# Writing out the group loop of an image-tower kernel on four engines

## The chip, the cores and the metric

The kernel runs on one core of a Trainium2 chip. The metric is the device time of one execution in microseconds (us), and of several runs the median. The core has four compute engines with an instruction stream each, TensorE (PE, the matrix unit), VectorE (DVE), ScalarE (ACT) and GpSimd (POOL), and SyncE (SP), which here issues most of the DMAs. Each stream is a program of its own: it has its own waits on semaphores, and its own branches if it has a loop.

## What is computed

Sixteen images of 3 x 256 x 256 pixels go through three steps:

```python
h = sum over channels of hypot(sobel_x(x), sobel_y(x))        # 16 x 256 x 256
h = concatenate([cls_tok, h])                                  # 257 tokens of 256 channels
y = layernorm(h)
h = h + attention(y)    # the 27 tokens of the greatest norm ask, 16 heads, all 257 answer;
                        # the other tokens get the mean of y
z = layernorm(h)
h = h + bit_linear(silu(depthwise_conv1d(bit_linear(z, w1))), w2)
```

`bit_linear` rounds its input to 8 bits row by row and its weights to -1, 0 and 1. The order of the additions and the roots are followed closely, so the gradient's length alone takes a chain of about 25 VectorE operations for two rows of pixels.

## The kernel before

The sixteen images are taken in four groups of four (`GROUPS = 4`, `GB = 4`). 128 partitions hold four images, 32 blocks of rows each; a partition has eight rows (`ROWS`), which are done in four pairs (`PAIRS`).

The work is software-pipelined over the groups. A head computes the gradients of group 0 and its norm. Then a **group loop** runs three passes (g = 1, 2, 3). A pass computes the gradients and the norm of group g, and between their steps the attention and the feed-forward part of group g - 1. A tail does attention and feed-forward of group 3. I call them pass 1, pass 2 and pass 3.

The loop stands in four streams, each with a counter in a register and a branch back at its end: on DVE (L1143), ACT (L1522), PE (L1828), and on SP (L457), where it has two passes only, since SP's first and last group are written out. GpSimd's stream has no loop. There is no barrier at the end of a pass: the streams meet only at semaphores. A semaphore counts up over the whole kernel, so inside the loop the value to wait for depends on the pass. It is worked out in a register, as in `Chain.__call__` (L107 to L111), which is used behind nearly every VectorE operation:

```python
    def __call__(self, ins):
        self.n += 1
        ins.then_inc(self.sem, 1)
        if self.n > self.lag:
            self.eng.wait_ge(self.sem, self.base + self.n - self.lag)
```

`base` is a number outside the loop and an expression of the register g inside it. The profile lists these register operations as ALU_OP and FUSED_REGOPS.

On DVE a pass is: `first_rows` (L1066, two operations on the image, L1069), `magnitude_rows` of pairs 0 and 1 with the attention of the previous group put in their slots (`slots_0`, `slots_1`), `attend`, `magnitude_rows` of pairs 2 and 3, `ffn_quantize`, `norm_tokens`, `ffn_result`. The last instruction of a pass is a one-column memset in `settle` (L521), which fills a gap; it writes the next free column of the scratch tile `idle`, which has 48. `selected_tokens` (L983) waits for the matmuls that gather the selected tokens (L1726), `own_heads` (L1014) for the weighted values (L1776, L1777), and `hypotenuse` starts with a wait for ACT's absolute values (L1238).

On ACT a pass begins with L1227, on PE with `attention` (L1701), after the copies of the transposed tokens (L1394). On SP a pass loads the next group's images, reloads weights, takes the token norms to DRAM and back, stores the previous group's output (`store`, L452, L454), and carries the slot numbers (L439 to L446).

A second, smaller loop of two passes in the tail (L1180 on DVE, L1549 on ACT) is not touched.

Of the kernel before, what the change touches and what calls it, by code (L numbers as in the profile page):

```python
# [44 lines left out]
GROUPS = B // GB  # L45
# [76 lines left out]
def tower_kernel(nc, x, cls_tok, w_in, b_qk, b_v, w_out, b_out, w1, conv_w, conv_b, w2, const, out):  # L122
# [9 lines left out]
    with ExitStack() as ctx:  # L132
# [238 lines left out]
        def load_rows(queue, g, b, lo, hi_, landed):  # L371

            block_rows, first = (slice(0, BLK), lo) if lo < ROWS else (slice(1, BLK + 1), lo - ROWS)
            src = x[bass.ds((g * GB + b) * CH, CH), block_rows, first:first + hi_ - lo, :].rearrange("c p r w -> p c r w")
            for c in range(CH):
                queue.dma_start(img[b * BLK:(b + 1) * BLK, c, lo:hi_, :], src[:, c]).then_inc(landed, 16)

        def load_images(queue, g):

            for b in range(GB):  # L380
                load_rows(queue, g, b, 0, ROWS, img_in)
                load_rows(queue, g, b, ROWS, ROWS + 2, img_in)
# [4 lines left out]
        @block.sync  # L387
        def _(sp):
            def load_weights():
                sp.dma_start(win[:, :, :], w_in.rearrange("(t p) n -> p t n", p=P)).then_inc(weights_in, 16)  # L390
                sp.dma_start(wout[:, :, :], w_out.rearrange("(t p) n -> p t n", p=P)).then_inc(weights_in, 16)

            for b in range(0, GB, 2):
                load_rows(sp, 0, b, 0, 3, img_first)
            sp.dma_start(cst[:, :], const).then_inc(table_in, 16)
            for b in range(0, GB, 2):
                load_rows(sp, 0, b, 3, 4, img_second)
            for b in range(GB):
                load_rows(sp, 0, b, 4, ROWS, img_in)
                load_rows(sp, 0, b, ROWS, ROWS + 2, img_in)  # L400
            sp.dma_start(h9[:, ROWS, :], cls_tok[0:1, :].to_broadcast([P, D])).then_inc(const_in, 16)
            sp.dma_start(stage.rearrange("p (t n) -> p t n", t=DT),
                         w1.rearrange("(t p) n -> p t n", p=P)).then_inc(w1_in, 16)
            sp.dma_start(stage2.rearrange("p (t n) -> p t n", t=FT),
                         w2.rearrange("(t p) n -> p t n", p=P)).then_inc(w2_in, 16)
            load_weights()
            sp.dma_start(bin_col[:, :], b_qk).then_inc(const_in, 16)
            sp.dma_start(bv_col[:, :], b_v).then_inc(const_in, 16)
            sp.dma_start(bo_row[:, :], b_out[0:1, :].to_broadcast([P, D])).then_inc(const_in, 16)
            sp.dma_start(cw[:, :, :], conv_w).then_inc(const_in, 16)  # L410
            sp.dma_start(cb[:, :], conv_b).then_inc(const_in, 16)

            def group(g, first=False, last=False):
                if first:
                    sp.wait_ge(stencil_psum, 2 * ROWS - 3)
                elif not last:
                    sp.wait_ge(mags, g * (2 * PAIRS) + 2 * PAIRS)
                if not last:
                    load_images(sp, g + 1)
                if not first:  # L420

                    sp.wait_ge(f_ready, g * GB)
                    load_weights()
                if first:

                    sp.wait_ge(e_ready, 1)
                    sp.dma_start(ec_dram, e9[0:1, ROWS:ROW9]).then_inc(e_out, 16)
                    sp.wait_ge(e_out, 16)
                    sp.dma_start(topk[:, 0, 0:1], ec_dram.to_broadcast([GB, 1])).then_inc(erow_in, 16)

                sp.wait_ge(e_ready, g + 1)
                sp.dma_start(e_dram, e9[:, 0:ROWS]).then_inc(e_out, 16)
                sp.wait_ge(e_out, g * 16 + 32)
                sp.dma_start(topk[:, 0, 1:S], e_dram.rearrange("(b r) j -> b (r j)", b=GB)).then_inc(erow_in, 16)
                if not first:
                    store(g - 1)

                sp.wait_ge(slots_ready, g + 1)
                sp.dma_start(s_dram.rearrange("(b r) j -> b (r j)", b=GB), topk[:, 4, 1:S]).then_inc(slots_out, 16)  # L439
                if not first:  # L440

                    sp.wait_ge(out_done, g * OUT_DONE)
                sp.dma_start(c_dram.rearrange("(b r) o -> b (r o)", b=GB), clsslot[:, :]).then_inc(slots_out, 16)
                sp.wait_ge(slots_out, g * 32 + 32)
                sp.dma_start(slot9[:, 0:ROWS], s_dram).then_inc(slot9_in, 16)
                sp.dma_start(slot9[:, ROWS:ROW9], c_dram).then_inc(slot9_in, 16)  # L446

            def store(g):

                sp.wait_ge(out_ready, g + 1)  # L450
                for b in range(GB):
                    sp.dma_start(out[bass.ds(g * GB + b, 1), 1:S, :].rearrange("o (p r) d -> (o p) r d", r=ROWS),  # L452
                                 out9[b * BLK:(b + 1) * BLK, 0:ROWS, :]).then_inc(out_done, 16)
                sp.dma_start(out[bass.ds(g * GB, GB), 0, :], out9[0:P:BLK, ROWS, :]).then_inc(out_done, 16)  # L454

            group(0, first=True)
            with sp.Fori(1, GROUPS - 1) as g:  # L457
                group(g)
            group(GROUPS - 1, last=True)
            store(GROUPS - 1)  # L460
            sp.wait_ge(out_done, GROUPS * OUT_DONE)
# [51 lines left out]
        def _(dve):  # L513
            v = nc.vector

            settled = [0]

            def settle():

                settled[0] += 1  # L520
                v.memset(idle[:, settled[0]:settled[0] + 1], 0.0)  # L521

            def bc(a, n):
# [57 lines left out]
            def norm_mean(step, rows, g):  # L581

                mean = small[:, 0, 0:rows]
                dve.wait_ge(rows_done, g * ROWS + ROWS + 2)
                ordered_sum(step, rows, h9[:, 0:rows, :], 16, mean)
                step(v.tensor_scalar(mean, mean, -1.0 / D, None, ALU.mult))
# [475 lines left out]
            def norm_tokens(step, g, rows, before_y=None):  # L1062
                norm_rows(step, rows, g * 2 + 1, before_y)
                dve.wait_ge(e_ready, g + 1)

            def first_rows(step, g):  # L1066
                dve.wait_ge(img_in, g * IMG_IN + IMG_IN)
                for f in range(2):
                    step(negative_edge_row(edge[:, f], f))  # L1069
                settle()  # L1070
# [69 lines left out]
            assert norm_step.n == NORM_STEPS - 1, norm_step.n  # L1140

            with dve.Fori(1, GROUPS) as g:  # L1143
                gl = g - 1
                norm_step = Chain(dve, vnorm, g * NORM_STEPS - 1)
                step = Chain(dve, vstep, gl * G_STEPS)
                first_rows(norm_step, g)
                magnitude_rows(g, 0, slots_0(step, gl))
                magnitude_rows(g, 1, slots_1(step, gl))
                attend(step, gl)  # L1150
                settle()
                for j in range(2):
                    magnitude_rows(g, 2 + j, lambda k: None)

                ffn_quantize(step, gl, range(GB), lambda: norm_mean(norm_step, ROWS, g),
                             lambda: norm_variance(norm_step, ROWS, g * 2 + 1))
                norm_tokens(norm_step, g, ROWS, lambda: dve.wait_ge(o_psum, gl * 5 + 5))
                ffn_result(step, gl)
                assert (norm_step.n, step.n) == (NORM_STEPS, G_STEPS), (norm_step.n, step.n)
# [32 lines left out]
        def _(act):  # L1192
# [326 lines left out]
                s.activation(clsT[:, t:t + 1], (A0, A1)[t][:, 0:1], ACT.Copy).then_inc(clsT_taken, 1)  # L1519

            tokens_transposed(0)
            with act.Fori(1, GROUPS) as g:  # L1522
                gl = g - 1
                magnitude_rows(g, 0, slots_0(gl))
                magnitude_rows(g, 1, slots_1(gl))
                attend(gl)
                tap_diagonals(gl)
                for j in range(2):
                    magnitude_rows(g, 2 + j, lambda k: ffn_take(gl, j, k))
                norm_squares(lambda j: ln[0][:, j, :], d_ready, g, ROWS)  # L1530
                ffn_scales(gl)
                first_root(g, ROWS)
                hidden_codes(gl)
                second_root(g, ROWS)
                tokens_transposed(g)
# [21 lines left out]
        def _(pe):  # L1557
# [267 lines left out]

            transposed(0)
            pe.wait_ge(bo_ready, 1)
            with pe.Fori(1, GROUPS) as g:  # L1828
                attention(g - 1)
                feed_forward(g - 1, convolve=True)  # L1830
                transposed(g, g * 5)
# [46 lines left out]
```

## Time and profile before

| | |
|---|---|
| median of 3 runs | 1610.13 us (1609.64 to 1610.77) |
| profiled execution, its own time | 1608.93 us |
| its span, first to last instruction | 1607.1 us |
| VectorE busy | 1383.6 us, 86% |
| TensorE matmul busy | 814.8 us, 51% |
| ScalarE busy | 700.1 us, 44% |
| mean granted TensorE clock | 0.706 |

The profile is of one execution, and its times run from the first instruction of the program. Register operations and branches do not count as busy time. "Idle before, issue" means that an engine stood still and no semaphore or transfer that the profile knows ended the wait. The clock is the share of full speed that TensorE was granted: 1.0 is 2.4 GHz, 0.5 is 1.2 GHz.

### The profile page before, as it was taken

What the parts mean: (1) busy time and instruction counts of PE and PEld (TensorE: products, weight loads), DVE (VectorE), ACT (ScalarE), POOL (GpSimd) and SP (SyncE); (2) the same over time, 40 slices, a digit from 0 to 9 for tenths busy, and PEclk for the clock granted to TensorE, in tenths of its full rate; (3) what the DMA queues carried; (4) which work ended last, traced back from release to release, by engine and by line L of the source; (5) the groups of instructions that cost most, each with busy time, mean ns of one, the idle gap of its engine ahead of it and who ended that gap; (6) DMA issues with size and microseconds to landing.
All of it is one profiled execution on the core that took longest, in us unless ns stands there. A gap on an engine that the chain in (4) does not pass through costs nothing.

```text
span 1607.1 us, 12610 instructions
## 1 busy us (share of the span) xinstructions
PE 814.8 (51%) x3262; PEld 639.7 (40%) x3262; DVE 1383.6 (86%) x2154; ACT 700.1 (44%) x1252; POOL 110.1 (7%) x154
## 2 busy tenths in 40 slices
PE   3466002465466733466447743356527754388543
PEld 1233001354354632355336532344426643276433
DVE  7999998999789999899879999899879999622676
ACT  2322241354456633254375544155356663143562
POOL 0000000010202000001101000002100100000000
PEclk7777556767579866667569876577568976677876
DMA  7001500030404510013303510104211300100001
GB/s 194 7 7 26 99 0 1 0 63 10 73 1 69 102 40 4 24 21 51 62 10 59 112 39 0 28 0 72 47 25 26 47 15 25 27 0 0 1 1 26
DMA packets 33976, 56.82 MB, mean 35 GB/s; under 512 B 6602, under 2 KB 23930, under 8 KB 32250
## 3 DMA queue, kind: packets, MB, share of 16 engines
q0 software_dynamic: 21024, 29.11, 11.2%
q1 hardware_dynamic: 12314, 26.31, 7.2%
q10 hardware_dynamic: 576, 0.79, 0.2%
q14 instruction: 49, 0.40, 0.1%
q8 instruction: 13, 0.21, 0.1%
HBM read 22.84 MB, written 4.25 MB: 17 GB/s over the span
## 4 chain that ended last, share of the span: by engine, by line
DVE 31%; issue 27%; ACT 15%; PE 12%; DMA 1%; DVEq 0%; SPq 0%; ACTq 0%
DVE arena L534 9%; DVE arena L531 6%; PE psum L1776 2%; ACT arena L1317 2%; DVE arena L903 2%; PE psum L1726 2%; PE psum L1630 1%; PE psum L1777 1%; PE psum L1812 1%; DVE red L547 1%; ACT arena L1453 1%; ACT arena L1200 1%; PE psum L1748 1%; DVE others L534 1%; ACT zT L1462 1%
## 5 line engine op out<-in xcount | busy, mean ns | idle before, releaser
L531 DVE TENSOR_TENSOR arena<-arena 128x768 f32<-128x768 f32 (+2 forms) x537 | 489.6, 967 | 24.8 <-ACT arena L1238 23.1
L534 DVE SCALAR_TENSOR_TENSOR arena<-arena 128x768 f32<-128x768 f32 (+2 forms) x224 | 201.5, 949 | 0.1
L1644 PE MATMUL psum<-zT,w1q 128*128 128x257 f32 x512 | 151.6, 435 | 40.9 <-ACT wout L1347 24.9
L1644 PEld LDWEIGHTS psum<-zT,w1q 128*128 128x128 f32 x512 | 112.1, 222 | 67.4 <-issue 27.3
L1630 PE MATMUL psum<-gpad,win 128*128 128x257 f32 x288 | 84.7, 437 | 54.6 <-ACT gpad L1329 54.6
L1269 ACT ACTIVATE arena<-arena 128x768 f32<-128x768 int16 x32 | 27.0, 843 | 174.9 <-DVE arena L534 174.4
L534 DVE SCALAR_TENSOR_TENSOR arena<-img 128x768 f32<-128x768 f32 x92 | 83.1, 950 | 16.4 <-DMA img<-x 8.6
L1748 PE MATMUL psum<-arena 128*128 128x257 f32 x128 | 51.0, 566 | 86.9 <-ACT arena L1436 65.7
L1630 PEld LDWEIGHTS psum<-gpad,win 128*128 128x128 f32 x288 | 62.3, 221 | 71.5 <-ACT gpad L1329 60.7
L507 POOL DMA_DIRECT2D h<-others x60 | 51.7, 862 | 404.4 <-DVE others L534 332.9
L1200 ACT ACTIVATE arena<-arena 128x256 f32<-128x256 f32 x65 | 23.3, 409 | 121.0 <-DVE arena L534 68.2
L1748 PEld LDWEIGHTS psum<-arena 128*128 128x128 f32 x128 | 34.8, 285 | 98.5 <-issue 83.8
L903 DVE TENSOR_REDUCE arena<-arena 128x288 f32<-128x2304 f32 (+1 forms) x16 | 64.5, 4086 | 0.1
L479 POOL DMA_DIRECT2D arena<-nrows_mem x18 | 15.6, 902 | 696.9 <-ACT arena L1248 533.4
L1776 PE MATMUL psum<-arena 128*128 128x64 f32 x256 | 55.0, 354 | 11.8 <-ACT arena L1436 11.8
L1426 ACT ACTIVATE arena<-psum,arena 128x257 f32<-128x257 f32 x64 | 29.5, 474 | 71.1 <-DVE arena L1002 71.1
L1336 ACT ACTIVATE xT<-psum,cb 128x257 f32<-128x257 f32 x96 | 43.6, 477 | 36.3 <-PE psum L1630 36.1
L534 DVE SCALAR_TENSOR_TENSOR arena<-arena,others 128x768 f32<-128x768 int16 x64 | 58.2, 949 | 0.0
L1726 PE MATMUL psum<-onehot,arena 128*128 128x128 f32 x128 | 24.2, 366 | 62.9 <-DVE arena L979 62.9
L1776 PEld LDWEIGHTS psum<-arena 128*128 128x128 f32 x256 | 47.7, 256 | 19.5 <-ACT arena L1436 13.6
L1317 ACT ACTIVATE arena<-xT 128x2048 f32<-128x2048 f32 (+1 forms) x14 | 55.3, 3951 | 0.3
L531 DVE TENSOR_TENSOR arena<-arena,img 128x768 f32<-128x768 f32 x59 | 53.9, 950 | 0.5
(225 smaller groups left out, 1980.7 us busy)
## 6 DMA issues: line engine op xcount, KB each, us to landing
img<-x SPq DMA_DIRECT2D x36, 258.0 KB, 6.9
h<-others POOLq DMA_DIRECT2D x60, 128.0 KB, 2.7
arena<-nrows_mem POOLq DMA_DIRECT2D x18, 384.0 KB, 4.4
arena<-arena POOLq DMA_DIRECT2D x18, 384.0 KB, 4.1
arena<-img POOLq DMA_DIRECT2D x18, 384.0 KB, 4.9
out<-out SPq DMA_DIRECT2D x16, 256.0 KB
img<-x SPq DMA_DIRECT2D x48, 64.5 KB, 5.9
win<-w_in SPq DMA_DIRECT2D x4, 768.0 KB, 5.5
```

The lines of the kernel that those rows point to most:

```text
L507: pool.dma_start(h9[:, row, :], others[:, row % 2, c, :], accum_op=ALU.add).then_inc(row_sums, 16)
L531: return v.tensor_tensor(o, a, b, op)
L534: return v.scalar_tensor_tensor(out=o, in0=a, scalar=s, in1=b, op0=op0, op1=op1)
L903: return v.tensor_reduce(fmax[:, :, bass.ds(b, 1), :].rearrange("p j o r -> p j (o r)"), f4[:, :, :, bass.ds(b, 1), :].rearrange("p t j o ...
L1200: ins = s.activation(ln[1][:, j, :], src(j), ACT.Square)
L1317: s.activation(fb[:, :, 0:ROWS, :], yd[:, :, 1:S].rearrange("p t (r j) -> p t j r", j=ROWS), ACT.Silu)
L1336: s.activation(ydw[:, t, :], (C0, C1, T0, T1)[i % 4][:, 0:S], ACT.Identity, bias=cb[:, t:t + 1]).then_inc(conv_taken, 1)
L1630: ins = mm((C0, C1, T0, T1)[i % 4][:, 0:S], diagonal(t, k), gpad[:, i % 4, k:k + S], start=(k == 0), stop=(k == 2))
L1644: ins = mm((A0, A1, B0, B1)[i % 4][:, 0:S], w1q[:, k, t * P:(t + 1) * P], zT[:, k, b, :], start=(k == 0), stop=(k == DT - 1))
L1726: ins = mm(C0[:, t * P:(t + 1) * P], y_row(j)[:, t * P:(t + 1) * P], rhs, start=(j == 0), stop=(j == ROWS))
L1748: mm((C0, C1, T0, T1)[hg][:, 0:S], qbd[:, hg // 2, 4 * (hg % 2):4 * (hg % 2) + 4, :].rearrange("p h q -> p (h q)"), kT[:, b % 2, hg // 2, ...
L1776: mm(B1[:, chans], attnT[:, f, m, cols], V[:, b % 2, m, chans], start=(m == 0), stop=False)
```

## The change

The three passes of the group loop are generated by a Python loop while the program is built, in place of a loop on the chip. Every pass has its own instructions then, and g is a number: each semaphore value and each address that was worked out in a register becomes a constant. The register operations, the counter and the branch back are gone from these four streams. Which compute operations and transfers there are, their order in each stream, and what each waits for stay as they were. Since `settle` is now called more often while the program is built, its column wraps around inside the 48 columns of `idle`.

```diff
@@ sync
             group(0, first=True)
-            with sp.Fori(1, GROUPS - 1) as g:
+            for g in range(1, GROUPS - 1):
                 group(g)
@@ vector
             def settle():
 
-                settled[0] += 1
+                settled[0] = settled[0] % 46 + 1
                 v.memset(idle[:, settled[0]:settled[0] + 1], 0.0)
@@ vector
-            with dve.Fori(1, GROUPS) as g:
+            for g in range(1, GROUPS):
                 gl = g - 1
@@ scalar
-            with act.Fori(1, GROUPS) as g:
+            for g in range(1, GROUPS):
                 gl = g - 1
@@ tensor
-            with pe.Fori(1, GROUPS) as g:
+            for g in range(1, GROUPS):
                 attention(g - 1)
```

## Rows read from the trace of the kernel before

**Rows 1.** The page, busy time, share of the span and instructions

```profile
PE 814.8 (51%) x3262; PEld 639.7 (40%) x3262; DVE 1383.6 (86%) x2154; ACT 700.1 (44%) x1252; POOL 110.1 (7%) x154
```

**Rows 2.** Windows: pass 1, pass 2, pass 3, tail; busy time, PE clock, DMA

```profile
274.40:641.30 366.90, 192.37 (x807) 157.07 (x808) 339.60 (x517) 178.19 (x329) 32.52 (x42) 0.72 0.22 39
641.30:1013.70 372.40, 198.73 (x803) 161.23 (x803) 339.56 (x517) 177.82 (x327) 32.53 (x42) 0.70 0.23 41
1013.70:1385.90 372.20, 199.55 (x804) 161.76 (x804) 339.65 (x517) 177.83 (x327) 32.53 (x42) 0.70 0.17 31
1385.90:1607.00 221.10, 132.97 (x598) 107.89 (x596) 111.13 (x235) 90.10 (x167) 0.00 (x0) 0.75 0.04 10
```

**Rows 3.** Timeline of DVE where a pass begins: start, length, [idle before <-releaser]

```profile
273.94 0.06 DVE L521 MEMSET idle<- 128x1 f32 x1
274.48 1.95 DVE L534 SCALAR_TENSOR_TENSOR arena<-img 128x768 f32<-128x768 f32 x2 [0.48 <-issue]
...
641.23 0.06 DVE L521 MEMSET idle<- 128x1 f32 x1
644.68 1.95 DVE L534 SCALAR_TENSOR_TENSOR arena<-img 128x768 f32<-128x768 f32 x2 [3.39 <-issue]
...
1385.83 0.25 DVE L521 MEMSET idle<- 128x1 f32 x2
```

**Rows 4.** The loop's line L1143: its branch, ns min/median/max

```profile
L1143 DVEq COMPARE_BRANCH  x3: 55/63/63, 641.3 to 1385.9; - x3
```

**Rows 5.** Instruction fetches by DMA queue: packets, MB; pass 1 (two rows), then pass 2

```profile
q8 instruction: 6, 0.10, 0.1%
q14 instruction: 12, 0.10, 0.1%
...
q14 instruction: 14, 0.11, 0.1%
```

**Rows 6.** Waits of DVE in pass 1 (two rows) and pass 2 (four): total, times, longest

```profile
DVE arena L531 <- PE psum L1777: 5.6, 1, 5.6
DVE arena L983 <- PE psum L1726: 0.5, 1, 0.5
...
DVE arena L531 <- PE psum L1777: 7.8, 2, 5.6
DVE arena L531 <- ACT arena L1238: 7.7, 2, 5.6
DVE arena L534 <- issue: 3.4, 1, 3.4
DVE arena L983 <- PE psum L1726: 1.4, 1, 1.4
```

**Rows 7.** Timeline of ACT and of PE where pass 2 begins

```profile
652.87 1.71 ACT L1227 ACTIVATE arena<-arena 128x768 f32<-128x768 f32 x2 [10.02 <-DVE arena L531]
...
642.98 3.36 PE L1701 MATMUL psum<-xT,win 128*128 128x257 f32 x7 [0.77 <-ACT xT L1394]
```

**Rows 8.** Timeline of SP in pass 2: the store, the slot numbers

```profile
641.38 2.75 SPq L452 DMA_DIRECT2D out<-out  x4
...
661.76 0.28 SPq L439 DMA_DIRECT2D s_dram<-nrows_mem  x1
```

**Rows 9.** Timeline of DVE at a wait that takes two register operations

```profile
327.34 0.17 DVE L1008 RECIPROCAL arena<-arena 128x4 f32<-128x4 f32 x1
327.54 0.42 DVE L531 TENSOR_TENSOR arena<-cst,arena 128x256 f32<-128x256 f32 x1
328.09 0.76 DVE L531 TENSOR_TENSOR arena<-arena,cst 128x256 f32<-128x256 f32 x2
```

**Rows 10.** Windows of the gathering matmuls (L1726): two of pass 1, one of pass 2

```profile
297.00:300.20 3.20, 2.94 (x14) 2.95 (x15) 3.20 (x5) 0.00 (x0) 0.00 (x0) 0.51 0.00 0
300.20:303.00 2.80, 2.80 (x27) 2.80 (x27) 2.26 (x4) 1.40 (x2) 0.00 (x0) 1.00 0.00 0
...
667.50:672.20 4.70, 4.69 (x22) 4.69 (x23) 4.70 (x6) 0.37 (x1) 0.00 (x0) 0.50 0.00 0
```

## The prediction

> **What bounds the kernel now.** I read the page first. VectorE is busy for 86% of the span, no other engine for more than 51% [rows 1]. That is an average, so the next view is the windows, cut at the points where the group loop begins, turns and ends. In each of the three passes VectorE works 339.6 us of 367 to 372, which is 91 to 93%; in the tail it works only 111 of 221 us and waits for PE and ACT [rows 2]. The passes make up 1111 of the 1607 us, and in them a microsecond of VectorE's time is a microsecond of the kernel's unless a later wait takes it back. The reader should also see that the three passes do the same work (517 VectorE instructions, 339.6 us each), yet the first is 5.5 us shorter than the second and the third [rows 2]. So this trace already holds an experiment: whatever the passes differ by is idle time.
>
> The third view is VectorE's timeline where a pass begins. Pass 1 is entered from above: the engine is idle for 0.48 us between the last memset and the first operation on the image. Pass 2 is entered by the branch back: 3.39 us idle, and pass 3, at 1017.05, has the same row with the same 3.39. The cause is given as "issue", so that no semaphore or transfer ended it. Where the loop is left by not branching, two memsets of 0.06 us take 0.25 us together, so some 0.13 us of it is idle [rows 3]. The branch itself is listed with 0.06 us at all three ends [rows 4]. The cost is therefore not in executing the branch but in what follows when it is taken: the stream has to begin again at instructions that it left hundreds of instructions ago. The DMA queues show that instructions are fetched from memory all the time, 12 packets in pass 1 and 14 in pass 2 on the queue that VectorE uses [rows 5].
>
> The Trainium skill says this outright (Runtime: NRT & Kernel Launch, section Instruction fetch mechanics): the sequencer streams instructions forward through two blocks, and a taken branch to a target outside of them must fetch it before anything goes on. The trace agrees: 3.39 us where the branch is taken, 0.13 us where it is not.
>
> **The change, part by part.**
>
> *The branch back on DVE.* Removed are three starts of a pass: 0.48 + 3.39 + 3.39 = 7.26 us, of which a straight stream should keep about 0.03 us each, the gap that stands between dependent operations elsewhere [rows 3, 9]. That is 7.2 us. The exit gives 0.1 us. Sum: 7.3 us.
>
> *The register operations on DVE.* Most are free: they run while the operation before them, usually one of 0.95 us, still computes. They cost something only behind a short operation and where two follow each other. The first operation of `queries` is such a place: 0.13 us idle against 0.03 us between the two operations ahead of it [rows 9]. There are three of these in each pass, for images 1, 2 and 3, so 9 x 0.10 = 0.9 us. Bounds: nothing, if the chain through PE and ACT that starts there ends later anyway, and 2 us if a few single gaps of the same size that I have not counted go too. I take 0.9.
>
> *The branches back on ACT and PE.* Cost nothing today, gain nothing. ACT's first operation of pass 2 starts at 652.87 after a wait of 10.02 us for VectorE's gradient, and PE's first starts when ACT has copied the last transposed tokens [rows 7]. What hides ACT's restart is VectorE's own start of the pass. After the change the gradient comes some 3.4 us earlier, and 10.0 - 3.4 = 6.6 us of cover are left, even if ACT's branch were still there.
>
> *SP.* It loses its branch and the register work ahead of each DMA. It is past four stores within 2.75 us, and the slot numbers that VectorE asks for leave at 661.76 [rows 8]. This transfer waits for VectorE's selection, so it moves up with it. Ahead of it on SP's queue stands a wait until the stores have landed. They were issued by 645.3; moving the selection up by 3.4 us leaves 13 us for them. Hidden on both sides, so 0, at most 0.1 us per pass.
>
> *More instructions to fetch.* PE's blocks were fetched six times in pass 1, and the queue is not listed at all in pass 2: its loop stayed on the chip [rows 5]. After the change passes 2 and 3 fetch them too, about 12 more packets. Price: nothing if they run ahead of PE, as in pass 1, which is the shortest pass. From above I have only the nearest row, 3.39 us for a fetch that nothing covers [rows 3]. I take 0, since pass 1 fetched for all engines and lost nothing by it.
>
> *The wrapped column of `idle`.* The same memset elsewhere: 0.
>
> *Where the time goes next.* When VectorE comes 3.4 us earlier into a pass, its partners come earlier too, since they wait for it. The waits that remain in a pass are chains that begin and end on VectorE: 7.7 us for L1238, 5.6 us for the last weighted values [rows 6]. Such waits keep their length.
>
> *TensorE's clock.* Here lies the greatest uncertainty. Two waits of pass 2 are longer than in pass 1: that for the gathering matmuls, 1.4 against 0.5 us, and those for the weighted values, 7.8 against 5.6 us [rows 6]. That is 3.1 us, and there are 5.5 - 2.9 = 2.6 us to explain beyond the branch. The work is the same; the clock is not. The gathering begins after a long idle time at the low level, 1.2 GHz, in both passes; it stays there for 3.2 us in pass 1, before the granted clock goes to 1.0, and for 4.7 us in pass 2 [rows 10]. Shifting every pass by a few us moves the bursts against these rises. I can't tell which way: passes 2 and 3 may win up to about 2.6 us each, pass 1 and the tail may lose as much each. I take 0.
>
> *Sum.* 7.3 + 0.9 = 8.2 us. The profiled execution took 1608.93 us, 1.8 us around its span of 1607.1, so its counterpart should take 1600.7. The median of the runs lay 1.2 us above the profiled one, which makes 1601.9 us.
>
> **Rivals.**
>
> *Larger, by the clock.* Passes 2 and 3 fall into the pattern of pass 1. Then 2 x 2.6 = 5.2 us come on top: 1596.7 us. For it: without the stall their beginning looks like that of pass 1. Against: the rises of the clock don't follow the pass.
>
> *The stall comes back as a wait.* Something that does not depend on VectorE ends last further on, and the 6.8 us of the two branches turn into longer waits for L1238 or L1777. Then only pass 1's entry and the register gaps remain, about 1609 us, and within 0.2% it is the same. Against it: pass 1 had no such stall, and its wait for the last weighted values is still 5.6 us, not 9 [rows 6].
>
> *Slower, by fetching.* The longer straight stream of PE, or of two engines that fetch at once, runs out of instructions. At 3.39 us for an uncovered fetch, three of them (10.2 us) outweigh the gain of 8.2, and six, one in two of PE's new ones, give 1610.1 - 8.2 + 20.3 = 1622 us. Against it stands pass 1, which fetched six for PE and is the shortest.
>
> *The branch is cheap and the 3.39 us are something else*, as the image's landing, for which the same instruction waits. By the branch's own 0.06 us [rows 4] two taken branches are worth 0.1 us, and with 0.9 for the registers the time would be 1609 us. Against it: the views give "issue", and the entry of pass 1, with the same wait, takes 0.48 us. The Trainium skill has figures of this kind (Advanced Engine Details and Errata, Control Flow Timing): about 51 ns for a plain branch and 108 ns for compare-and-branch. By these alone the sum would shrink to about 0.2 us for the branches, no measurable change.
>
> **How the numbers follow.** This measurement can tell about 0.2%, 3.2 us, from no change. Gain of 5 to 11 us as summed: 0.6. More than that by the clock: 0.16. Gain of 3.2 to 5 us, when the clock takes some back: 0.07. Stall returns as a wait, or the clock takes nearly all: 0.09. Branch cheap: 0.02. Fetching makes it slower: 0.06. So faster 0.83, same 0.11, slower 0.06. The time is that of the sum, 1601.9 us. Its lower end adds the clock's 5.2 us and another 2.6 in the tail: 1594. Its upper end loses 2.6 us in pass 1 and 2.6 in the tail: 1607. Below and above are left some 2 in 10. The likeliest case's own range is 1599 to 1605.
>
> **What the profile after would show.** VectorE goes from the last memset of a pass into the first image operation without a gap of "issue". The first operation of `queries` follows after 0.03 us. VectorE's busy time stays at 1383 us, and the idle time falls by about 8. Passes 2 and 3 become about 369 us. ALU_OP and FUSED_REGOPS are all but gone; PE's queue of fetches is busy in all three passes. The prediction is wrong if there are new gaps of "issue" inside a pass on DVE or PE, if the waits for L1238 or for the weighted values have grown by 3 us, or if those for PE have changed by more than 5 us in sum, because its clock rose at other moments.

## The result and the profile after

The changed kernel takes 1597.7 us, median of 4 runs (1596.8 to 1598.0), against 1610.45 us (1609.6 to 1611.5) of the kernel before. The ratio is 0.992, with an interval of 0.9902 to 0.9937. That is 12.7 us less, where 8.2 were forecast (8.5 to the time itself): faster, inside the range of 1594 to 1607, and 4.2 us beyond the forecast time of 1601.9. By the two profiled executions it is 1607.1 - 1596.2 = 10.9 us of span; the rest is that the profiled run of before lay 1.5 us below its median, and that of after 0.3 above.

The page of the changed kernel, its first lines and the fetch queues:

```profile
span 1596.2 us, 11035 instructions
PE 821.6 (51%) x3262; PEld 645.2 (40%) x3262; DVE 1383.0 (87%) x2154; ACT 700.1 (44%) x1252; POOL 110.5 (7%) x154
...
q8 instruction: 26, 0.43, 0.1%
q14 instruction: 32, 0.26, 0.1%
```

VectorE, ScalarE and GpSimd are as busy as in [rows 1] to within 0.6 us, and all operation counts are the same. Only TensorE differs, 821.6 us against 814.8 for the same 3262 matmuls: its work meets the clock at other moments. On VectorE, which bounds the passes, only idle time can have gone. Next the windows, cut as in [rows 2] near the points where VectorE enters a pass or the tail:

```profile
274.00:641.20 367.20, 197.09 (x807) 160.51 (x807) 339.26 (x516) 178.82 (x330) 32.55 (x42) 0.71 0.22 39
641.20:1009.80 368.60, 199.09 (x803) 162.30 (x803) 339.46 (x517) 177.57 (x327) 32.55 (x42) 0.70 0.23 42
1009.80:1378.10 368.30, 199.42 (x803) 162.79 (x804) 339.41 (x520) 177.64 (x327) 32.81 (x42) 0.70 0.18 31
1378.10:1596.20 218.10, 133.79 (x598) 107.44 (x598) 111.08 (x236) 90.17 (x167) 0.00 (x0) 0.74 0.04 10
```

Passes 2 and 3 went from 372.4 and 372.2 us to 368.6 and 368.3. Pass 1 did not gain, 367.2 against 366.9. (The gap at its entry lies ahead of both windows. From its first image operation, at 273.80, pass 1 takes 367.4 us up to the entry of pass 2; before the change it took 366.8 up to the branch.) The tail, which the change doesn't touch, went from 221.1 to 218.1. The reader should stop at this last row: 3 of the 10.9 us come from a stretch whose instructions are the same.

VectorE's timeline where pass 2 begins, with the rows that answer to [rows 3]:

```profile
641.11 0.06 DVE L944 MEMSET small<- 128x1 f32 x1
641.21 0.95 DVE L534 SCALAR_TENSOR_TENSOR arena<-img 128x768 f32<-128x768 f32 x1
641.24 0.06 DVE L521 MEMSET idle<- 128x1 f32 x1
```

The image operation starts 0.04 us behind the memset of L944. The 3.39 us are gone. The profile lists the last memset of the pass (L521) inside the image operation now; it had stood in front of it, so that from the end of L944's memset to the image operation the time went from 3.51 to 0.04 us. ScalarE's first operation of pass 2, and two operations of VectorE at the place of [rows 9]:

```profile
649.40 1.71 ACT L1227 ACTIVATE arena<-arena 128x768 f32<-128x768 f32 x2 [6.48 <-DVE arena L531]
```

```profile
327.09 0.42 DVE L531 TENSOR_TENSOR arena<-cst,arena 128x256 f32<-128x256 f32 x1
327.55 0.76 DVE L531 TENSOR_TENSOR arena<-arena,cst 128x256 f32<-128x256 f32 x2
```

ScalarE now waits 6.48 us for VectorE's gradient instead of 10.02 [rows 7]; the prediction had 6.6 us of cover left. The gap ahead of `queries` is 0.04 us, where it was 0.13.

VectorE's waits in pass 2, which answer to [rows 6]:

```profile
DVE arena L531 <- PE psum L1777: 7.7, 2, 5.6
DVE arena L531 <- ACT arena L1238: 7.7, 2, 5.5
...
DVE arena L983 <- PE psum L1726: 1.3, 1, 1.3
```

They are what they were, 7.8, 7.7 and 1.4 us. No wait took the stall's place.

The prediction named new gaps of "issue" inside a pass on PE as a sign that it is wrong, and there is one in every pass, at L1748. Here is that of pass 1, in the kernel before and in the changed one:

```profile
310.32 3.71 PE L1748 MATMUL psum<-arena 128*128 128x257 f32 x8 [5.53 <-DVE arena L531]
```

```profile
309.84 3.77 PE L1748 MATMUL psum<-arena 128*128 128x257 f32 x8 [5.50 <-issue]
```

PE stands still as long as before, 5.50 against 5.53 us. Only the cause that the profile puts down has changed, so this is no new gap. PE's idle time ahead of L1748 is 84.9 us in the whole kernel, where it was 86.9.

### The profile page after: what moved, and what is told of

It is laid out like the page before. It is cut to its first block, busy times and chain, and to the rows that moved or that the text cites. A ratio compares the mean times of both kernels' runs of the same rounds, so it can differ in the third digit from the quotient of the medians.

```text
span 1596.2 us, 11035 instructions
## 1 busy us (share of the span) xinstructions
PE 821.6 (51%) x3262; PEld 645.2 (40%) x3262; DVE 1383.0 (87%) x2154; ACT 700.1 (44%) x1252; POOL 110.5 (7%) x154
## 4 chain that ended last, share of the span: by engine, by line
DVE 49%; PE 14%; ACT 13%; issue 8%; DMA 1%; SPq 0%; DVEq 0%; ACTq 0%
DVE arena L531 18%; DVE arena L534 13%; DVE arena L903 3%; PE psum L1630 2%; PE psum L1776 2%; PE psum L1726 2%; ACT arena L1200 1%; PE psum L1644 1%; PE psum L1748 1%; PE psum L1777 1%; ACT arena L1317 1%; PE psum L1812 1%; DVE red L547 1%; ACT arena L1453 1%; ACT zT L1462 1%
## 5 line engine op out<-in xcount | busy, mean ns | idle before, releaser
L1748 PE MATMUL psum<-arena 128*128 128x257 f32 x128 | 53.8, 592 | 84.9 <-ACT arena L1436 66.5
L1748 PEld LDWEIGHTS psum<-arena 128*128 128x128 f32 x128 | 36.4, 298 | 96.9 <-ACT arena L1436 70.3
L1776 PE MATMUL psum<-arena 128*128 128x64 f32 x256 | 56.2, 360 | 11.8 <-ACT arena L1436 11.8
L1776 PEld LDWEIGHTS psum<-arena 128*128 128x128 f32 x256 | 49.0, 262 | 19.7 <-ACT arena L1436 13.6
L534 DVE SCALAR_TENSOR_TENSOR arena<-arena,small 128x256 f32<-128x256 f32 x131 | 53.3, 480 | 0.6
```

What stands on the lines that cost most here:

```text
L534: return v.scalar_tensor_tensor(out=o, in0=a, scalar=s, in1=b, op0=op0, op1=op1)
L1748: mm((C0, C1, T0, T1)[hg][:, 0:S], qbd[:, hg // 2, 4 * (hg % 2):4 * (hg % 2) + 4, :].rearrange("p h q -> p (h q)"), kT[:, b % 2, hg // 2, ...
L1776: mm(B1[:, chans], attnT[:, f, m, cols], V[:, b % 2, m, chans], start=(m == 0), stop=False)
```

## The experiments

Unless said otherwise each kernel was timed in turn with the kernel before on the same chip, 3 rounds or more. Over all of these runs the kernel before took 1607.5 to 1612.1 us, with medians of 1609.9 to 1610.3. A single run thus scatters by some 2 us each way, so medians that are less than 2 us apart are told apart only by their traces.

### VectorE alone

```diff
-            with dve.Fori(1, GROUPS) as g:
+            for g in range(1, GROUPS):
```

with `settle` as in the change; ACT, PE and SP keep their loops.

> Only VectorE's passes are written out; PE, ACT and SP keep their loops, registers and branches. My theory (the gain is VectorE's, where the taken branch stopped it) expects nearly the whole gain: a time within 2 us of the 1597.7 us of the full change, and VectorE's passes entered without a gap. The rival that the other three streams' branches or register work share in the gain expects 1600 us or more.

It took 1602.7 us (1600.7 to 1604.1), ratio 0.9957 (0.9943 to 0.9971). VectorE has no gap of "issue" left where a pass begins. The gain is 7.6 us, about my sum of 8.2, but 5 us short of the full change. By what I had written down, that spoke for the rival: the other streams seemed to share in the gain.

### All but VectorE

> The reverse: PE, ACT and SP written out, VectorE keeps its loop. My theory expects no gain that can be measured, 1609 to 1611 us, with VectorE's two gaps of 3.39 us still there. The rival expects 2 us or more below the kernel before, 1608 us or less.

It took 1610.3 us (1609.2 to 1612.1), ratio 1.0003 (0.9993 to 1.0012). Writing out PE, ACT and SP is worth nothing by itself. VectorE's waits in it name the loop's stall, now 4.1 us at its longest; the two branches back cost 4.08 and 4.03 us, where I had expected 3.39 each:

```profile
DVE arena L534 <- issue: 8.6, 3, 4.1
```

No run says why this stall grew. The result of no gain therefore holds 1.3 us of longer stalls, which something else in the kernel made up for.

So 7.6 and 0 us in two halves, and 12.7 us together: something that is no sum of parts is at work. The last experiments go after that.

### A hint in place of writing out

```diff
-            with dve.Fori(1, GROUPS) as g:
+            with nc.Fori(1, GROUPS, engines=bass.OrderedEngineSet([dve.engine]), hint_back_edge=True) as g:
```

It took 1601.9 us (1599.8 to 1605.1), ratio 0.9947 (0.993 to 0.9965). VectorE's sequencer at the loop's line, and its timeline where pass 2 begins:

```profile
L1143 DVEq BRANCH_PREFETCH_HINT  x3: 39/39/61, 274.4 to 1018.3; - x3
...
L1143 DVEq COMPARE_BRANCH  x3: 61/68/90, 645.7 to 1386.4; - x3
```

```profile
645.66 0.06 DVE L521 MEMSET idle<- 128x1 f32 x1
646.51 1.95 DVE L534 SCALAR_TENSOR_TENSOR arena<-img 128x768 f32<-128x768 f32 x2 [0.80 <-issue]
```

Loop, counter, registers and branch are all there, and the stall is 0.80 us where it was 3.39. The branch is as long as before, 0.07 us. That shows what the stall was: the fetch of the branch's target, which the hint orders ahead of time. The cheap-branch rival falls with it: the image had landed long before (in the kernel before, the last load ahead of pass 2 was issued at 537.0 us, and none of them took more than 9.2 us to land), and nothing about the image differs between these two kernels.

The size of the gain is another matter. VectorE's three entries (0.60, 0.80 and 0.74 us for 0.48, 3.39 and 3.39) account for 5.1 of the 8.4 us by which the median lies below that of the kernel before. The tail of this trace is 4.3 us shorter, which is the subject of a later section.

### Branches that are not taken

```diff
+            for p in range(1, GROUPS):
+                with dve.Fori(p, p + 1) as g:
+                    one_pass(g)
```

> VectorE's three passes as three loops of one trip each: every pass has its own instructions and no branch is taken, but g stays in a register and all register operations stay. PE, ACT and SP as before. It separates the branch from the register work. My sum (branch 7.3, registers 0.9 us) expects it about 1 us above the run with VectorE written out; if the register work carries the part of the gain that I did not foresee, it is 3 to 5 us above it.

It took 1602.2 us (1602.0 to 1603.8), the same as VectorE written out (1602.7). A branch that is there and isn't taken leaves 0.20 us idle or less, against 3.39. As a test of the registers it failed: for a loop of one trip the builder puts g in as a constant. The profile shows 54 ALU_OPs at L111 in this kernel, as in the one with VectorE written out, where the kernel before has 873.

Its trace also has PE's own stall in the open: PE, whose loop is kept, stands still for 3.04 us of "issue" at its first matmul of pass 3 (L1704, at 1014.18). The time is none the worse for it, which fits a restart of PE that is hidden behind VectorE.

### Registers kept, branches gone

```diff
+            regs = nc.alloc_registers("g_pass", engines=bass.OrderedEngineSet([dve.engine]))
+            nc.regs_mov(regs, 1)
+            for p in range(1, GROUPS):
+                one_pass(nc.snap(regs, min_val=1, max_val=GROUPS - 1))
+                nc.regs_alu(regs, regs, 1, op=ALU.add)
```

> VectorE's three passes written out, but g stays in a register that is counted up between them, so that every register operation of the loop is still there and every branch is gone. PE, ACT and SP as before the change. (The single trips of the run before it had let the builder fold g into constants.) My sum expects it 0.9 us above the run with VectorE written out with constants (1602.7 us), 1603 to 1604 us, and the gaps of 0.13 us in front of the first operation of queries. The rival that register work is worth several us expects 1606 us or more.

It took 1603.6 us (1601.4 to 1604.6). VectorE's register operations at L111, and its timeline at `queries`:

```profile
L111 DVEq ALU_OP  x873: 40/40/57, 274.8 to 1556.8; - x175
```

```profile
328.76 0.42 DVE L531 TENSOR_TENSOR arena<-cst,arena 128x256 f32<-128x256 f32 x1
329.32 0.76 DVE L531 TENSOR_TENSOR arena<-arena,cst 128x256 f32<-128x256 f32 x2
```

All 873 operations are there, and so is the gap of 0.14 us. The median is 0.9 us above that of VectorE written out, which is my term, but the two sets of runs overlap nearly whole. The traces settle it better. Added up over a pass, VectorE's short gaps (under 0.15 us, those that no wait explains) come to 4.4 us in every kernel that keeps VectorE's registers, this one and the one with the hint among them, and to 3.9 or 4.0 us in every kernel where g is a number. (Pass 1 of the kernel before has 4.5.) That is 1.4 us in three passes, of which 0.2 stand where the passes meet. So 873 register operations of 0.04 us, 35 us in sum, cost 1.2 to 1.4 us and not several. They run while the operation ahead of them computes.

The entry of pass 1 is the same 0.48 us here as in the kernel before, with no loop and no branch. What stands in it in both is a MOVE and a FUSED_REGOPS, so that gap belongs to setting up the register and not to a fetch.

### The stall put back

```diff
+            def pause(ns):
+
+                n = -(-ns // 840)
+                w = round((ns / n - 69) / 1.0417)
+                for k in range(n):
+                    v.tensor_reduce(pad[:, k:k + 1], cst[:, 0:w], AX, ALU.add)
...
             for g in range(1, GROUPS):
                 gl = g - 1
+                if g > 1:
+                    pause(3370)
```

`pad` is a view of the scratch tile `red`, which is free there. The changed kernel itself was timed again beside it.

> The changed kernel once more, beside the next three on one chip, as their reference. All theories expect 1597 to 1599 us again. If it comes out at 1601 us or more, then the gain beyond my sum was a matter of the chip or the day and not of the kernel.

> The changed kernel, with reductions that nobody reads, about 3.4 us of VectorE's time, at the beginning of passes 2 and 3: the two stalls put back without a branch or a register. If the stalls on VectorE carry the gain, it loses most of it, 6.7 us more than the changed kernel, 1604 to 1605 us, and by the clock up to 1608. If later waits swallowed a stall of this kind, it stays within 2 us of the changed kernel.

The changed kernel took 1598.2 us (1597.5 to 1603.9), the one with the stall put back 1604.0 (1602.8 to 1606.1): 5.8 us for 6.7 put in. One of the four runs of the repeat took 1603.9, so its ratio to the kernel before is wide, 0.9942 (0.9919 to 0.9965), and reaches up to that of VectorE alone (0.9957); its median is 11.8 us below the kernel before, where the first measurement gave 12.7. The windows of passes 2 and 3 with the stall put back:

```profile
640.80:1012.40 371.60, 196.96 (x803) 160.12 (x803) 342.88 (x523) 177.82 (x327) 32.55 (x42) 0.70 0.23 42
1012.40:1383.60 371.20, 197.95 (x803) 161.30 (x804) 342.89 (x524) 177.29 (x327) 32.53 (x42) 0.70 0.17 31
```

Against the changed kernel's 368.6 and 368.3 us they are 3.0 and 2.9 longer, by 3.4 us of added work. A stall at the head of a pass goes into the time nearly whole, also when useless work makes it.

### Where most of the other 5 us are: work put in ahead of the tail

The tail kept coming back in two sizes. In ten traces it took 220.6 to 221.4 us (the kernel before, the three in which only VectorE's passes are straight, and the one with PE, ACT and SP written out alone) or 216.1 to 218.1 (the changed kernel and its repeat, the one with the stall put back, the one with 2.0 us ahead of the tail below, and the one with the hint). It has the same instructions in all ten and VectorE works 111 us in it. The streams that are written out don't sort these, since the hint's kernel has every loop and a tail of 216.8. So I moved the tail in time and changed nothing else:

```diff
             gl = GROUPS - 1
             step = Chain(dve, vstep, gl * G_STEPS)
+            pause(2000)
             select(step, gl)
```

The changed kernel with 2000 and with 1000, and the kernel with VectorE alone written out with 1300:

> The changed kernel, with three reductions of a constant tile that nobody reads put on VectorE ahead of the tail, about 2.0 us. By plain addition it takes 2.0 us more than the changed kernel, and the tail keeps its 218.1 us. If the tail's length hangs on where its matmul bursts fall against the rises of TensorE's clock, its length from the first selection to the end changes by 1 us or more, up or down, with the same work in it.

> The changed kernel (1597.7 and 1598.2 us, tail 218.1 and 217.4 us) with about 1.0 us put on VectorE ahead of the tail; 2.0 us there had cost the profiled span nothing. By the theory of the clock this one may fall on the long side: a tail of about 221 us behind the pause and 1601 to 1602 us in all, more than with 2.0 us put in. Plain addition expects 1599 us, less than with 2.0 us.

> Only VectorE's passes written out (1602.7 us, its tail 221.3 us in the profile), with two reductions that nobody reads, about 1.3 us, put on VectorE ahead of the tail. In ten traces so far the tail took either 220.7 to 221.4 us or 216.1 to 218.1 us, with the same work, and which of them went with where its beginning fell against the moments at which TensorE's clock changes. By those traces 1.3 us more turn this kernel's tail into a short one: about 216.5 us behind the pause, a profiled span of about 1597.5 us, and a median near 1599 to 1601 us, that is, added work makes it faster. If the tail's length had to do with which streams are written out, it stays at 221 us and the kernel takes 1604 us.

What differs is the clock under PE's work. From 35 to 50 us into the tail PE is busy almost without a pause in all of these kernels, with attention matmuls that VectorE's next steps wait for. The windows of these 15 us, in the kernel before, with VectorE alone written out, and in the changed kernel with 1.0 us ahead, which have the long tail (the column before the last two is the granted clock):

```profile
1421.00:1436.00 15.00, 15.00 (x44) 12.31 (x45) 1.82 (x3) 2.88 (x10) 0.00 (x0) 0.50 0.01 1
```

```profile
1414.60:1429.60 15.00, 15.00 (x51) 12.50 (x51) 1.82 (x3) 2.89 (x10) 0.00 (x0) 0.57 0.00 1
```

```profile
1414.10:1429.10 15.00, 15.00 (x44) 12.31 (x45) 1.82 (x3) 2.89 (x10) 0.00 (x0) 0.50 0.00 0
```

And in the changed kernel, with VectorE alone written out and 1.3 us ahead, and in the changed kernel with 2.0 us ahead, which have the short one:

```profile
1413.00:1428.00 15.00, 15.00 (x60) 12.40 (x61) 2.49 (x6) 3.68 (x12) 0.00 (x0) 0.67 0.00 0
```

```profile
1417.40:1432.40 15.00, 14.24 (x65) 11.75 (x64) 3.23 (x8) 5.03 (x14) 0.00 (x0) 0.77 0.01 1
```

```profile
1414.70:1429.70 15.00, 14.24 (x66) 11.76 (x65) 3.23 (x8) 5.02 (x14) 0.00 (x0) 0.77 0.00 1
```

At 0.50 and 0.57 these 15 us hold 44 to 51 matmuls, at 0.67 and 0.77 they hold 60 to 66. The same 24 matmuls of the weighted values (L1776 and L1777 in the kernel before) take 6.6 us from first to last in the first three kernels and 4.0 to 4.1 in the other three. The clock's average over a longer stretch does not tell the two kinds apart: over the first 50 us it is 0.73 in the kernel before, with a long tail, and 0.72 in the changed kernel, with a short one. The kernel before has its high clock partly where PE has nothing to do, as from 1391 to 1396 us, with 0.98 and not one matmul.

| kernel | tail behind the pause, us | profiled span, us | median, us |
|---|---|---|---|
| VectorE alone | 221.3 | 1600.9 | 1602.7 |
| VectorE alone, 1.3 us put in | 216.6 | 1599.0 | 1598.65 (1598.4 to 1600.8) |
| changed kernel | 218.1, again 217.4 | 1596.2, 1595.7 | 1597.7, 1598.2 |
| changed, 1.0 us put in | 220.6 | 1599.7 | 1600.2 (1597.5 to 1601.7) |
| changed, 2.0 us put in | 216.1 | 1595.9 | 1599.6 (1597.7 to 1601.0) |

With 1.3 us of useless work the kernel with VectorE alone written out became 4 us faster by the medians, and reached the changed kernel. The two sets were taken on different chips, each beside the kernel before (1610.3 and 1610.0 us); the ratios are 0.9957 (0.9943 to 0.9971) and 0.9931 (0.9917 to 0.9945), so their intervals just touch. The tail of 216.6 us was forecast as 216.5, and what PE and ACT could gain as a head start on VectorE is no more than the 1.3 us of the pause, against 4.7 us. The profiled span of 1599.0 is longer than the 1597.5 that I expected, since the three passes of that execution took 1.4 us more than those of the same code without the pause. In the changed kernel 1.0 us ahead made the tail 3 us longer in the trace, as forecast, and 2.0 us cost the trace nothing. By the medians these last two can't be told apart (1600.2 and 1599.6), and the first is below the 1601 to 1602 that I had expected: probably runs of one kernel don't all begin the tail at the same point, so that a median mixes both kinds, but only one execution of each kernel has a trace.

### The short loop of the tail, and the hint on three engines

The first kernel is the changed one with the tail's loop written out as well. The second is the kernel before with the hint on the group loops of VectorE, ScalarE and PE.

```diff
-            with dve.Fori(0, 2) as j:
+            for j in range(2):
...
-            with act.Fori(0, 2) as j:
+            for j in range(2):
```

> The changed kernel with the short loop of the tail written out as well, on VectorE and ScalarE. There the taken branch costs VectorE nothing that shows and ScalarE 0.23 us, since the loop is short. The theory that only a branch back to code that has to be fetched again is dear expects no change beyond 0.3 us plus the clock's scatter: 1597 to 1599 us. If a taken branch were dear as such, 3 us less: 1595 us.

> The kernel before with the hint at the head of the group loop on VectorE, ScalarE and PE, and nothing written out. The theory that only VectorE's restart is on the path expects the same as with the hint on VectorE alone, 1601.9 us, give or take 2 us. If ScalarE's and PE's restarts had a share, it comes near the changed kernel, 1598 us.

The hint on three engines took 1601.55 us (1599.5 to 1603.1), as on VectorE alone (1601.9). So ScalarE's and PE's restarts are hidden behind VectorE's.

The kernel with the tail's loop written out too is the fastest of all: 1596.8 us (1596.1 to 1599.0), ratio 0.9925 (0.9909 to 0.994) to the kernel before. Against the changed kernel's 1597.7 and 1598.2 the difference is within the scatter, but the trace has a cause that I had missed. ScalarE at the turn of that loop, in the changed kernel and then with the loop written out:

```profile
1524.22 0.20 ACT L1320 ACTIVATE idle<-clsT 128x1 f32<-128x1 f32 x1
1524.67 1.28 ACT L1356 ACT_TABLE_LOAD   x1 [0.25 <-issue]
1525.97 1.09 ACT L1356 ACTIVATE xT<-gpad,cb,cw 128x257 f32<-128x257 f32 x2
```

```profile
1523.85 0.20 ACT L1320 ACTIVATE idle<-clsT 128x1 f32<-128x1 f32 x1
1524.02 1.09 ACT L1356 ACTIVATE xT<-gpad,cb,cw 128x257 f32<-128x257 f32 x2
```

VectorE's first operation that waits for this, in the same two kernels:

```profile
1526.61 1.77 DVE L534 SCALAR_TENSOR_TENSOR xT<-gpad,cw,xT 128x257 f32<-128x257 f32 x4 [2.01 <-ACT xT L1356]
```

```profile
1524.66 1.77 DVE L534 SCALAR_TENSOR_TENSOR xT<-gpad,cw,xT 128x257 f32<-128x257 f32 x4 [0.34 <-ACT xT L1356]
```

The branch itself is cheap here, 0.25 us. The body of this loop is short, one turn in 34 us; that this is the reason is likely, but no run varies it. But the head of the loop holds a load of ScalarE's function table of 1.28 us. The straight code doesn't have it, and its wait is 1.7 us shorter. My expectation of no change beyond 0.3 us had left this out.

## Why the prediction was right, and where its size was off

The time lies in the range, but not in its likeliest part. The gain of 12.7 us is above the 5 to 11 us that had a chance of 0.6, and 1597.7 is below the 1599 to 1605 of that case. It landed where the rival "larger, by the clock" stood, with a chance of 0.16, and not by that rival's mechanism: passes 2 and 3 did not fall into the pattern of pass 1. What gained was the tail, which the prediction knew only as a possible loss. That part of the result is luck.

In the two traces the 10.9 us are made up as follows: 7.7 where the passes meet, 1.3 in short gaps of the register work, 3.0 in the tail and 0.4 in small differences of busy time and the head; and 1.5 us are lost, since VectorE's longer waits in the passes grew from 72.6 to 74.1 us in sum, nearly all of it in pass 1.

**VectorE's idle time at the pass starts: right.** 7.3 us were forecast, and 7.7 went. The gaps of 0.48, 3.39 and 3.39 us became 0.04 or 0.05 each. The exit gained 0.2 and not 0.1, and each of the three entries gave 0.1 more, for the memset that had stood in the way. The hint shows that the two gaps of 3.39 us were the fetch of the target. That of 0.48 us, which the prediction put among the branches, was the setting up of the register, since it stays with registers kept and branches gone. The account of the Trainium skill (Runtime: NRT & Kernel Launch, section Instruction fetch mechanics) agrees with both traces. The Trainium skill's figures that pointed the other way (Advanced Engine Details and Errata, Control Flow Timing) are 51 ns for a plain branch and 108 ns for compare-and-branch. The branch here is a compare-and-branch, and its own record is 55 to 63 ns, so the second figure is too high for it; and neither says anything of the 3.3 us behind the record.

**That no later wait takes it back: right.** The waits of pass 2 kept their length, and 3.4 us put back by other means came out as 3.0 and 2.9. VectorE's waits for PE, which the prediction allowed to change by 5 us in sum, went from 112.2 to 111.8.

**ScalarE, PE and SP cost nothing: right,** by the kernel with all but VectorE written out (1.0003, with VectorE's stalls 1.3 us longer in it), and for ScalarE and PE by the two kernels with the hint.

**Registers, 0.9 us: right in kind, a little small.** The gaps went as said. The sum of the short gaps puts them at 1.2 to 1.4 us in the three passes, so there were more places than the nine that the prediction counted; its upper bound was 2 us. The medians alone, 0.9 us apart with ranges that overlap, would not show it.

**Fetching a longer stream costs nothing: right.** PE's queue has 26 packets where its loop had 13, VectorE's share a queue that went from 49 to 32, and no new gap appears on VectorE or PE; PE's 5.50 us of "issue" at L1748 stood there before under another name.

**The clock, taken as 0: this term was mis-sized.** It was 0 in the sum, with 2.6 us per pass and for the tail as bounds. The 2.6 us themselves were misread. The window of pass 1 in [rows 2] begins at 274.40, so it leaves out the 0.48 us at its entry, and taking 2.9 us off the 5.5 counts them twice: without the stall, passes 2 and 3 took 369.0 us each and pass 1 took 366.8, a difference of 2.2. Measured, the passes gave nothing: passes 2 and 3 did not take pass 1's pattern, pass 1 took theirs (its wait for L1777 went from 5.6 to 7.7 us in sum), and VectorE's waits of pass 1 grew by 1.3 us. The tail gave 3.0 us in the profiled pair. I had treated the tail as a bound on one side only, a loss.

The 5 us between VectorE alone and the full change are this in the main. Of the 4.7 us between their traces the tail has 3.2, and the trace with 1.3 us put in shows that its length hangs on where it begins: it brought the tail from 221.3 to 216.6 us and the median from 1602.7 to 1598.65. The other 1.5 us are about what the passes of one and the same code differ by from one execution to the next, 1.4 us. I have no kernel that moves the phase of pass 1, so what made its waits grow is put down to the clock by argument alone.

**The scatter between runs.** My basis was a profiled run 1.2 us under the median of three. Over 9 to 14 runs the kernel before spreads over 4 to 5 us. Some 1.8 us of the 12.7 are this.

## What to carry to other kernels

Look at the bound engine's timeline where a loop turns: a gap of "issue" there that is small or missing where the loop is entered and left is likely the fetch of the target, and a hint that makes it shrink shows it. Here it cost 3.4 us per taken branch, and only on the engine that bounds. Writing out that one stream gives it back, and a hint at the loop's head, which leaves the code as short as it was, gives back all but 0.8 us of it. When two halves of a change don't add up to the whole, look for a stretch that neither of them touches and move it in time by a microsecond or two before explaining the difference by the code.

## What the runs showed of the hardware that I had not expected

- A tail of 221 us with the same instructions becomes one of 216 when it begins 1.3 us later, because TensorE's clock is high at other points of its bursts: 0.57 and 51 matmuls against 0.77 and 65 in the same 15 us; 2.0 us of added work were free in the trace.
- A hinted branch back leaves 0.80 us idle, one that isn't taken 0.13 to 0.20, an unhinted one to a far target 3.39, and 4.08 once PE, ACT and SP are written out.
- A loop's head on ScalarE may hold a table load of 1.28 us that the same code written out doesn't need.
- 873 register operations on VectorE, 35 us in sum, cost 1.2 to 1.4 us.
